# Token attention with the values as the stationary side: one kernel of four transformer stages, one change

## The reference

```python
def _L2_attn_ref(x, qkv_w, proj_w, proj_b, temperature):
    qkv = (x @ qkv_w.T).reshape(B, N, 3, H, Dh)           # H = 6 heads of Dh = 16
    q, k, v = ...
    attn = jnp.einsum('bhnd,bhmd->bhnm', q, k) / C ** 0.5 / temperature
    attn = jnp.where(diag, -jnp.inf, attn)
    attn = jax.nn.softmax(attn, axis=-1)
    out = jnp.einsum('bhnm,bhmd->bhnd', attn, v)
    return out.transpose(0, 2, 1, 3).reshape(B, N, C) @ proj_w.T + proj_b

def _L3_attn_ref(x, w_qkv, w_proj, b_proj):
    ...
    scores = jnp.einsum('bhqd,bhkd->bhqk', q, k) * HEAD_SIZE ** (-0.5)
    scores = jnp.where(causal, scores, -inf)              # causal: tril
    out = softmax(scores) @ v                             # then the projection, as above
```

## Time and profile before

| | us |
|---|---|
| median of 3 runs | 1125.86 (1125.4 to 1127.91) |
| span of the profiled execution | 1127.2 |
| token attention, layer 2: first scores to last add | 370.93 to 562.33 |
| experts, layer 2 | about 567 to 735 |
| token attention, layer 3: steady rounds | 770 to 925 |
| TensorE busy in the whole span | 958.1 (85%) |
| VectorE, ScalarE, POOL busy | 573.5, 437.1, 352.6 |

### The profile page before, as it was taken

How to read it: one execution, slowest core, us unless ns; L and a number is a source line. 1 busy time by engine, 2 the same in 40 slices (tenths; PEclk the granted TensorE clock), 3 DMA queues, 4 the chain that set the end, 5 groups by cost and what they waited for, 6 DMA issues and landing times. The chain is left out here.

```text
span 1127.2 us, 19914 instructions
## 1 busy us (share of the span) xinstructions
PE 958.1 (85%) x6512; PEld 845.9 (75%) x6512; DVE 573.5 (51%) x1736; ACT 437.1 (39%) x698; POOL 352.6 (31%) x386
## 2 busy tenths in 40 slices
PE   1787777689983799999979999957999997999998
PEld 1655555389982599888869999936888886888887
DVE  5766565320044477666435656434766753444442
ACT  1243434320022334443255455522344333555453
POOL 4223323290003222331143533432234134233432
PEclk9986887679985799999979999966999997999999
DMA  3700000000102434322000000014343410000000
GB/s 71 109 12 0 0 0 0 1 4 15 15 1 46 87 80 86 82 63 64 1 1 0 0 0 0 1 42 91 91 91 72 93 26 1 9 7 13 8 7 15
DMA packets 28969, 36.76 MB, mean 33 GB/s; under 512 B 10696, under 2 KB 25856, under 8 KB 28928
## 3 DMA queue, kind: packets, MB, share of 16 engines
q1 hardware_dynamic: 28928, 36.24, 15.6%
HBM read 25.06 MB, written 11.17 MB: 32 GB/s over the span
## 5 line engine op out<-in xcount | busy, mean ns | idle before, releaser
L1413 PE MATMUL ps<-w,ff_b_h 128*128 128x96 f32 x1536 | 181.8, 275 | 6.7 <-ACT ff_b_fT L1469 6.7
L1413 PEld LDWEIGHTS ps<-w,ff_b_h 128*128 128x128 f32 x1536 | 178.5, 192 | 10.5 <-issue 7.3
L1480 ACT ACTIVATE ff_b_h<-ps,b 128x512 f32<-128x512 f32 x192 | 128.8, 687 | 121.5 <-PE ps L1405 121.3
L1016 PE MATMUL ps<-values,at_b_pT 128*128 128x102 f32 x1344 | 161.7, 276 | 1.0 <-POOL at_b_pT L941 0.4
L1016 PEld LDWEIGHTS ps<-values,at_b_pT 128*128 128x128 f32 x1344 | 155.2, 192 | 3.3 <-issue 1.4
L941 POOL TENSOR_SCALAR_AFFINE_SELECT at_b_pT<-at_b_pT 128x768 f32<-128x768 f32 x64 | 54.6, 865 | 237.3 <-ACT at_b_pT L1126 236.6
L1553 DVE SCALAR_TENSOR_TENSOR tok<-ps,ff_b_gate,tok 128x96 f32 (+1 forms) x224 | 56.0, 312 | 136.1 <-PE ps L1413 136.1
L1189 DVE TENSOR_REDUCE at_b_mf<-ps 128x6 f32<-128x1536 f32 (+1 forms) x64 | 98.1, 1552 | 25.5 <-PE ps L993 25.0
L614 DVE SCALAR_TENSOR_TENSOR ca_qk<-ca_raw,dw,ca_qk 96x225 f32<-96x225 f32 (+1 forms) x256 | 98.8, 451 | 0.0
L1126 ACT ACTIVATE at_b_pT<-ps 128x1536 f32<-128x1536 f32 x64 | 80.9, 1291 | 43.7 <-PE ps L1001 43.5
L991 PE MATMUL ps<-keys,at_b_qs 96*128 96x256 bf16 (+1 forms) x384 | 70.8, 272 | 22.6 <-issue 20.0
(11 more groups left out here) (224 smaller groups left out, 1557.8 us busy)
## 6 DMA issues: line engine op xcount, KB each, us to landing
at_parts<-at_b_part SPq DMA_DIRECT2D x96, 96.0 KB
at_b_qs<-at_parts SPq DMA_DIRECT2D x16, 288.0 KB, 4.2
keys<-at_parts SPq DMA_DIRECT2D x16, 288.0 KB, 5.4
at_b_qs<-at_parts SPq DMA_DIRECT2D x16, 192.0 KB, 5.8
keys<-at_parts SPq DMA_DIRECT2D x16, 192.0 KB, 6.3
w<-in_L_ffn_w SPq DMA_DIRECT2D x4, 576.0 KB
chan<-in_x SPq DMA_DIRECT2D x4, 384.0 KB, 5.5
windows<-lines_d SPq DMA_DIRECT2D x96, 13.0 KB, 1.6
```

What stands on the lines that cost most here:

```text
L1016: ins = nc.tensor.matmul(ps[:, 6 + u, OW * t:OW * (t + 1)], pT[:, u, k, h, P * t:P * (t + 1)], vp[:, slot, u, k, h, :], start=(n == 0), st ...
L1413: ins = nc.tensor.matmul(ps[:, 6 + e % 2, C * t:C * (t + 1)], h[:, e % 2, j, P * t:P * (t + 1)], f.w2[:, e * HC + j, :], start=(j == 0), s ...
L1480: nc.scalar.activation(h[:, e % 2, j, :], ps[:, 3 * (e % 2) + j, :], ACT.Gelu, bias=f.b1[:, e * HC + j:e * HC + j + 1]).then_inc(s_h, 1)
```

## The change

The two sides of the weighted values are swapped. The stationary side becomes `vp` of one head, now 32 columns wide (16 values and 16 ones), the moving side `pT` with 256 queries. The result of a head stands on 32 partitions (16 of values, 16 of sums), with the queries along the free side. Heads 0 to 3 stand on the four groups of 32 output partitions, in columns 0 to 255 of the bank. Heads 4 and 5 are done per tile of 128 queries, on the four groups once more, in columns 256 to 383. The loop over `weighted_values` runs over key tiles k instead of query tiles t, and each k waits only for its own mask. In layer 3 the second key tile has only 128 queries.

ScalarE then copies the bank's 384 columns to SBUF (`sums`), and TensorE turns them back with three transposes (`spread`), the last with a strided output, so that queries are on the partitions again and each head has 32 columns: 16 of output, then sums. VectorE's `out` reads its divisor from the first of the ones as before. `vp` no longer needs zeros between the blocks: it is set to ones once.

In the order, both blocks of image 0 now stand before the queries of pair i + 2 instead of one on each side of queries and values; `spread` stands where `turn_out` and the second block stood; `turn_out` and `project` of image 0 move down; VectorE's `out(i, 0)` moves from before the maxima to between the first two reductions, and `add(i - 1, 0)` from behind the first reduction to behind the third. ScalarE gets two copies a round.

```diff
@@ -27,9 +27,9 @@
 GN_CH = 3
 CA_H, CA_D = 8, 12
 H, D = 6, 16
-VD = D + 1
+VB = 2 * D
 MAX_ROWS = 3 * H
-OW = H * VD
+OB = TPI * H * VB
 Q = 4 * P
 E, HID = 4, 384
 HC = HID // P
@@ -106,7 +106,7 @@
 
 
     m.ks = sb("keys", [C + MAX_ROWS, 2, H, 2, N], BF16)
-    m.vp = sb("values", [P, 2, 2, TPI, H, OW])
+    m.vp = sb("values", [P, 2, 2, TPI, H, VB])
     m.mxp = sb("maxima", [P, 2, TPI, C + MAX_ROWS], BF16)
     m.oT = sb("outT", [C + 1, 2, N])
     m.vec = sb("vec", [C, NV])
@@ -805,11 +805,7 @@
                                     base=-H * k, pattern=[[-1, H], [0, 2], [0, N]], channel_multiplier=1))
     link(pool.memset(m.oT[C:C + 1, :, :], 1.0))
     link(pool.memset(m.mxp[:, :, :, :], 0.0))
-    link(pool.memset(m.vp[:, :, :, :, :, :], 0.0))
-    for slot in range(2):
-        for k in range(2 * TPI):
-            blocks = m.vp[:, slot, k // TPI, k % TPI, :, :].rearrange("p h w -> p (h w)")
-            link(pool.memset(bass.AP(blocks.tensor, blocks.offset + D, [blocks.ap[0], [OW + VD, H], [1, 1]]), 1.0))
+    link(pool.memset(m.vp[:, :, :, :, :, :], 1.0))
 
 
 def token_rstd(m, pool, i, n, s_rstd, s_mv=None):
@@ -1008,15 +1005,30 @@
                         ins = nc.tensor.transpose(turned_max[:, P * t:P * (t + 1)], mxp[:, u, t, :], m.ident_b[:, :])
                     ins.then_inc(s_M, 1)
 
-                def weighted_values(i, slot, u, t):
-                    if t == 0:
-                        pe.wait_ge(s_zero, 4 * i + 2 * u + 2)
-                    terms = [(k, h) for k in range(1 if causal and t == 0 else TPI) for h in range(H)]
-                    for n, (k, h) in enumerate(terms):
-                        ins = nc.tensor.matmul(ps[:, 6 + u, OW * t:OW * (t + 1)], pT[:, u, k, h, P * t:P * (t + 1)],
-                                               vp[:, slot, u, k, h, :], start=(n == 0), stop=(n == len(terms) - 1))
-                    if t == TPI - 1:
-                        ins.then_inc(s_O, 1)
+                def weighted_values(i, slot, u, k):
+                    pe.wait_ge(s_zero, 4 * i + 2 * u + k + 1)
+                    n0 = P if causal and k == 1 else 0
+                    for h in range(4):
+                        nc.tensor.matmul(ps[VB * h:VB * (h + 1), 6 + u, n0:N], vp[:, slot, u, k, h, :], pT[:, u, k, h, n0:N],
+                                         start=(k == 0), stop=(k == TPI - 1), skip_group_check=True)
+                    for t in range(n0 // P, TPI):
+                        for h in range(4, H):
+                            q = 2 * t + h - 4
+                            ins = nc.tensor.matmul(ps[VB * q:VB * (q + 1), 6 + u, N:N + P], vp[:, slot, u, k, h, :],
+                                                   pT[:, u, k, h, P * t:P * (t + 1)], start=False,
+                                                   stop=(k == TPI - 1 or (causal and t == 0)), skip_group_check=True)
+                    if k == TPI - 1:
+                        ins.then_inc(s_U, 1)
+                def spread(i, u):
+                    pe.wait_ge(s_uc, 2 * i + u + 1)
+                    w = OB // TPI
+                    for t in range(TPI):
+                        nc.tensor.transpose(ps[:, 6 + u, w * t:w * t + P], uo[:, u, P * t:P * (t + 1)], m.ident[:, :])
+                    nc.tensor.transpose(ps[:, 6 + u, 0:OB].rearrange("p (t n) -> p t n", t=TPI)[:, :, P:w],
+                                        uo[:, u, N:N + P], m.ident[:, :]).then_inc(s_O, 1)
 
                 def turn_out(i, u):
                     pe.wait_ge(s_on, 2 * i + u + 1)
@@ -1038,21 +1050,24 @@
                     pe.wait_ge(s_vp, 2 * i + 1)
                     scores(i, slot, 0, 0)
                     if back:
-                        turn_out(i - 1, 0)
+                        spread(i - 1, 0)
                     pe.wait_ge(s_vp, 2 * i + 2)
                     scores(i, slot, 0, 1)
                     if back:
-                        project(i - 1, 0)
                         weighted_values(i - 1, 1 - slot, 1, 0)
+                        turn_out(i - 1, 0)
                     pe.wait_ge(s_mx, 4 * i + 1)
                     scores(i, slot, 1, 0)
                     if back:
-                        pe.wait_ge(s_tk, 2 * i - 1)
+                        weighted_values(i - 1, 1 - slot, 1, 1)
+                        project(i - 1, 0)
                     pe.wait_ge(s_mx, 4 * i + 2)
                     scores(i, slot, 1, 1)
+                    if back:
+                        pe.wait_ge(s_tk, 2 * i - 1)
                     turn_maxima(i, 0)
                     if back:
-                        weighted_values(i - 1, 1 - slot, 1, 1)
+                        spread(i - 1, 1)
                     pe.wait_ge(s_mx, 4 * i + 3)
                     pe.wait_ge(s_mr0, i + 1)
                     transposed_scores(i, slot, 0, 0)
@@ -1076,12 +1091,12 @@
                     if ahead == 2:
                         pe.wait_ge(s_xT, i + 3)
                     weighted_values(i, slot, 0, 0)
+                    weighted_values(i, slot, 0, 1)
                     pe.wait_ge(s_ex, 4 * i + 4)
                     if ahead == 2:
                         queries_keys(i + 2, slot)
                     if ahead:
                         values(i + 1, 1 - slot)
-                    weighted_values(i, slot, 0, 1)
 
                 turn(first)
                 queries_keys(first, 0)
@@ -1099,8 +1114,10 @@
                 back_and_front(end - 1, 1)
                 middle(end - 1, 1, 0)
                 weighted_values(end - 1, 1, 1, 0)
+                spread(end - 1, 0)
+                weighted_values(end - 1, 1, 1, 1)
                 turn_out(end - 1, 0)
-                weighted_values(end - 1, 1, 1, 1)
+                spread(end - 1, 1)
                 project(end - 1, 0)
                 turn_out(end - 1, 1)
                 project(end - 1, 1)
@@ -1129,6 +1146,10 @@
                     act.wait_ge(s_M, 2 * i + 1)
                     nc.scalar.copy(qs[C:KR, slot, :, 0, :], max_rows()).then_inc(s_mr0, 1)
 
+                def sums(i, u):
+                    act.wait_ge(s_U, 2 * i + u + 1)
+                    nc.scalar.copy(uo[:, u, :], ps[:, 6 + u, 0:OB]).then_inc(s_uc, 1)
                 def out(i, u):
                     act.wait_ge(s_OT, 2 * i + u + 1)
                     nc.scalar.copy(oT[0:C, u, :], ps[0:C, 6 + u, 0:N]).then_inc(s_oT, 1)
@@ -1136,9 +1157,14 @@
                 def step(i, slot, ahead):
 
                     weights(i, 1)
+                    sums(i, 0)
                     if ahead == 2:
                         parts(i + 2)
-                    out(i, 0)
+                    if ahead:
+                        out(i, 0)
+                    sums(i, 1)
+                    if not ahead:
+                        out(i, 0)
                     if ahead:
                         rows(i + 1, 1 - slot)
                         weights(i + 1, 0, (0,))
@@ -1179,7 +1205,7 @@
                         for t in range(TPI):
                             blocks = vp[:, slot, u, t, :, :].rearrange("p h w -> p (h w)")
                             ins = nc.vector.tensor_copy(
-                                bass.AP(blocks.tensor, blocks.offset, [blocks.ap[0], [OW + VD, H], [1, D]]),
+                                bass.AP(blocks.tensor, blocks.offset, [blocks.ap[0], [VB, H], [1, D]]),
                                 ps[:, 3 * u + 1, C * t:C * (t + 1)].rearrange("p (h d) -> p h d", d=D))
                         ins.then_inc(s_vp, 1)
 
@@ -1208,7 +1234,7 @@
 
                 def out(i, u):
                     dve.wait_ge(s_O, 2 * i + u + 1)
-                    o = ps[:, 6 + u, 0:TPI * OW].rearrange("p (t h w) -> p t h w", t=TPI, h=H)
+                    o = ps[:, 6 + u, 0:OB].rearrange("p (t h w) -> p t h w", t=TPI, h=H)
                     nc.vector.reciprocal(rec[:, u, :, :], o[:, :, :, D]).then_inc(s_rc, 1)
                     dve.wait_ge(s_rc, 2 * i + u + 1)
                     nc.vector.tensor_tensor(on[:, u, :, :].rearrange("p t (h d) -> p t h d", d=D), o[:, :, :, 0:D],
@@ -1229,10 +1255,12 @@
                     back = i is not first
                     maximum(i, 0, 0)
                     if back:
-                        add(i - 1, 0)
+                        out(i - 1, 0)
                     maximum(i, 0, 1)
                     maxima_parts(i, 0)
                     maximum(i, 1, 0)
+                    if back:
+                        add(i - 1, 0)
                     maximum(i, 1, 1)
                     maxima_parts(i, 1)
                     if back:
```

5 lines of the change are left out of this document (3 added, 2 removed).

## The result

| | before | after |
|---|---|---|
| median of 20 runs, us | 1126.08 (1122.54 to 1131.27) | 1119.64 (1113.23 to 1129.35) |
| ratio to before, 95% interval | | 0.995 [0.9928, 0.9971] |
| span of the profiled execution, us | 1127.2 | 1114.5 |

The change makes the kernel faster by 0.5%, about 6 us. The forecast of 1131 us, slower than before, was wrong in its sign; the time lies in the range. The two spans differ by 12.7 us, twice as much. So half of the 12.7 us is the choice of executions, and where the rows don't name the place of a gain it may be that.

The account below looks back on a forecast made before the run. TensorE's list looked like the bound, with nearly everything around the blocks a chain through other engines. 25 us saved and 30 us lost to a falling clock gave +5 us: 1131 us, range 1098 to 1190.

Parts of the forecast that it names:

- The walk: One layer 2 attention round followed station by station along its chain of waits: 1.1 us a round gained at full clock.
- The end of layer 2: Layer 2's last round and tail after its last queries: gains of 3.5 us and about 4.5 us.
- the 25 us of the sum: Rounds and ends of both token attentions at unchanged clock, less ScalarE copies: 25 us less.
- The price of the block: TensorE's new weighted-values block: 1.3 us, between 0.65 (four at a time) and 2.6 (no overlap).
- case A: The forecast itself: column groups overlap in part, clock falls in most rounds; 1118 to 1146 us, chance 0.38.
- some 2.5 us: Slack of TensorE's list against VectorE's in a round, set against the work lost at half clock.
- the point from which the list decides: Block price of about 1.8 us, where the chain and TensorE's list are equally long.
- the term of 30 us for the clock: TensorE's idle time makes its clock fall in most token attention rounds: 2.1 us a round, 14 rounds, 30 us lost.
- B: TensorE's clock holds in the token attentions, so the saving stays: 1096 to 1114 us, chance 0.27.
- C: TensorE's clock stays low over long stretches and TensorE becomes the bound: 1146 to 1186 us, chance 0.10.
- D: No overlap between column groups, a block costs 2.6 us: 1168 to 1206 us, chance 0.20.
- E: ScalarE's new copies delay query casts and row copy, 13 of 25 us given back, clock held: 1114 us, chance 0.05.

Follow-up runs that it names:

- experiment 2: The kernel after, with 36 unread fill matmuls on TensorE before the first scores and 20 before the second spread: 1107.28 us.
- Experiment 5: The kernel after, with every matmul of a weighted-values block issued twice, no fills: 1138.80 us.
- Experiment 11: The kernel after, with every matmul of a block issued twice and 36 and 20 unread fill matmuls on TensorE: 1120.81 us.
- experiments 6 and 7: The kernel after, with each block matmul issued four times: 1207.50 us; the kernel after, with each ScalarE copy of the sums made twice: 1121.73 us.

## Why the prediction was wrong

**The walk was right.** Station by station, at full clock, predicted and measured in layer 2: queries to scores 5.4 and 5.63, to turned maxima 8.0 and 8.00, to transposed scores 1.8 and 1.84, the last part 3.7 and 3.70. The gain of 1.1 us a round is 0.8. In layer 3 0.9 was said and 1.3 measured (20.91 to 19.64). Twelve rounds: 12 said, 12.4 by these. The idle time of 2.5 us before the scores is 2.80. The end of layer 2 was to give 8.0 and gave 8.2; that of layer 3, 6 and 4.5. These parts add up to 25.1. In the medians, with the clock held, the 25 us of the sum are 18.6 (experiment 2); where the rest stays isn't shown.

**The price of the block failed, and with it the sign.** It was taken at 1.3, between 0.65 and 2.6, and is 0.68. The reason given was that the second instruction of a matmul waits for the first, in a queue that starts in order; eight instructions of 256 columns start within 0.46 us (505.07 to 505.53) where 0.216 apiece had been read the earlier trace rows, so four groups do run side by side. Experiment 5 is the kernel that the forecast described, with a block of 1.3 and the falling clock. It takes 1138.80 us, inside the 1118 to 1146 that case A had, and slower than before. The kernel after differs from it in that price alone and is faster than before. That its own 1119.64 us also lies in A's range is luck, since A is the case of the dearer block. In the prediction's sum the price enters through the room in TensorE's list, of which "some 2.5 us" were to be left against VectorE's; four blocks at 0.68 instead of 1.3 leave 2.5 us more. The Trainium skill, TensorE: Matmul & The Clock Gate, Part 3, lets column tiles run concurrently; the trace agrees, and more strongly than by the 2.38x that the page gives for three (four groups here: 8 x 0.216 + 8 x 0.108 = 2.6 us of work in 0.68, 3.8x).

**The forecast's 5 us were also two errors against each other.** With the block at 1.3 the prediction held the list of TensorE for covered: 25 us less at full clock. Experiment 11 shows 6.5 less (1120.81 against 1127.29). The step that failed is that a saving of 5 us of list a round leaves room everywhere in it: behind the second reduction in layer 3 and behind the exponentials in both layers TensorE had less room than a block more. The prediction put the point from which the list decides at about 1.8 us a block; at 1.3 it already costs 13.5 us. The other error is the term of 30 us for the clock, 2.1 a round in all 14: it is 18.0 with the block at 1.3 (experiment 5 against 11), and 12.4, 0.9 a round, in the kernel after (against experiment 2). So at the price that the forecast took its sum of -25 + 30 should have been -6.5 + 18.0. In the profiled execution it falls in four of five rounds of layer 2 and three of five of layer 3, so the frequency was nearly right, but its 2.1 was taken between stretches of 7 us (1.0) and of 13 us (4). Five of the seven have only 3.4 us at half clock, which in layer 2 costs 0.5 to 0.6 us and in layer 3 1.4 to 1.6; the two with 6.8 us cost 1.6 to 1.8, and none of 13 us occurs in these rounds.

**The rivals.** B (the clock holds, 1096 to 1114) isn't the case, since the clock is at 0.92 in both windows; the time with the clock held by fills, 1107.28, lies in its range. C isn't seen: the longest stretch at half clock in a steady round of after is 6.8 us. D and E are answered by experiments 6 and 7: D's price is real (1207.50, just over its range), its premise false; E's copies are covered. What I had no case for is after itself: full overlap and a clock that falls in part. By experiment 2 the 6 us measured are -18.6 + 12.4 = -6.2; the sum closes by construction, since both terms are differences to the same run. The rows that the prediction named for it (0.65 for a block, granted clock 0.8 to 0.95 in the window of layer 2, scores 5.4 us after the queries (5.63 measured), transposed scores released by the row copy) all came out so, but in no one case's combination.

**TensorE's change of tiling.** The Trainium skill, TensorEngine Tiling (Array Packing), Key Properties, says that a change of tiling mode drains the engine. The rows don't show a drain as such, but they bound its cost: a block followed by untiled matmuls takes 0.79 us (495.19 to 495.98) and one followed by a block 0.68. So leaving the tiles costs about 0.1 us, if this is its cost. There are six changes a round and not the eight of the prediction, since the two blocks of image 0 stand together: an estimate of 0.6 us of TensorE's list from these rows.

```profile
495.19 0.64 PE L1013 MATMUL ps<-at_b_pT,values 128*32 128x256 f32 x8
495.64 0.40 PE L1018 MATMUL ps<-at_b_pT,values 128*32 128x128 f32 x8
495.98 0.69 PE L1042 MATMUL ps<-wT,outT 97*128 97x96 f32 x4
```
